# A one-element memset and a wait for it after every second indirect DMA of GpSimd

## What is computed

```python
edge_index = jnp.stack([src, dst])
x = x + _L0_gnn_ref(_layernorm(x), edge_index, W, a)            # graph attention
x = x + _L0_ffn_ref(_layernorm(x)[None], ...)[0]                # top 1 of 32 experts
x = x + _L1_gnn_ref(_layernorm(x), edge_attr_8, edge_attr_4, ..., edge_index)
x = x + _L1_ffn_ref(_layernorm(x)[None], ...)[0]                # top 2 of 6 experts
x = x + _L2_gnn_ref(_layernorm(x), src, dst, ...)               # Q, K, V attention on edges
x = x + _L2_ffn_ref(_layernorm(x)[None], ...)[0]                # 8 experts, dense
x = x + _L3_gnn_ref(_layernorm(x), W, att, src, dst)            # attention of 4 heads
x = x + _L3_ffn_ref(_layernorm(x)[None], ...)[0]                # top 2 of 8 experts
```

```python
z = jnp.einsum('nd,hdf->nhf', h, W)
e = jax.nn.leaky_relu(es[src] + ed[dst], SLOPE)
ex = jnp.exp(e - m[dst])
alpha = ex / safe                                               # safe: sum of ex per target
out = jax.ops.segment_sum(alpha[:, :, None] * z[src], dst, num_segments=N)
```

## Time and profile before

| | us |
|---|---|
| median of 3 runs | 5434.05 |
| fastest and slowest run | 5420.24, 5452.84 |
| span of the profiled execution | 5506.1 |
| PE busy in it | 3864.8 (70%) |
| DVE busy | 3234.8 (59%) |
| ACT busy | 2686.0 (49%) |
| POOL busy, 2641 instructions | 2546.9 (46%) |

### The profile page before, as it was taken

How to read it: one execution, slowest core, us unless ns; L and a number is a source line. 1 busy time by engine, 2 the same in 40 slices (tenths; PEclk the granted TensorE clock), 3 DMA queues, 4 the chain that set the end, 5 groups by cost and what they waited for, 6 DMA issues and landing times.

```text
span 5506.1 us, 74255 instructions
## 1 busy us (share of the span) xinstructions
PE 3864.8 (70%) x19152; PEld 2551.9 (46%) x19152; DVE 3234.8 (59%) x8314; ACT 2686.0 (49%) x8902; POOL 2546.9 (46%) x2641
## 2 busy tenths in 40 slices
PE   5767888822428999977766666668999936556665
PEld 2336656612314444456634444445555524444454
DVE  7864666514246889876566777764333335555753
ACT  5644666611116888863335555553333325555521
POOL 5655555553346777713425555532000046666234
PEclk8977898855668999988878888889999966677778
DMA  3013232312223333323335555550000023333334
GB/s 116 22 45 82 76 77 78 76 15 64 78 63 91 89 86 88 85 25 110 109 124 147 145 150 142 147 133 1 6 12 12 10 80 82 87 86 88 38 112 131
DMA packets 278819, 441.36 MB, mean 80 GB/s; under 512 B 114083, under 2 KB 192781, under 8 KB 278157
## 3 DMA queue, kind: packets, MB, share of 16 engines
q0 software_dynamic: 124624, 331.70, 23.7%
q1 hardware_dynamic: 147230, 98.37, 6.2%
q10 hardware_dynamic: 6560, 6.55, 0.4%
HBM read 368.84 MB, written 67.60 MB: 79 GB/s over the span
## 4 chain that ended last, share of the span: by engine, by line
PE 49%; DVE 16%; another core or an unknown queue 15%; issue 9%; ACT 7%; DMA 2%; DVEq 1%; POOL 0%; ACTq 0%; SPq 0%; POOLq 0%
PE PB L3144 6%; PE PB L2528 6%; PE PB L726 5%; PE PB L1998 5%; PE PB L1079 4%; PE PB L3128 3%; ACT XNT L2612 2%; PE PB L2008 2%; PE PB L1574 2%; PE PB L1088 1%; PE PB L1562 1%; DVE bigt L705 1%; PE PB L2020 1%; PE PB L2015 1%
## 5 line engine op out<-in xcount | busy, mean ns | idle before, releaser
L2528 PE MATMUL PB<-XNT 128*128 128x260 f32 x1760 | 605.0, 480 | 115.8 <-DVE bigt L2500 51.7
L2646 POOL DMA_INDIRECT bigt<-ZTAB,DO x440 | 459.8, 1045 | 270.7 <-issue 122.7
L1023 POOL DMA_INDIRECT bigt<-HTAB,bigt x440 | 419.9, 954 | 350.3 <-ACT bigt L1109 203.5
L1970 POOL DMA_INDIRECT bigt<-YTAB,bigt x440 | 469.4, 1067 | 141.7 <-issue 128.3
L717 ACT ACTIVATE bigt<-bigt 128x128 f16<-128x128 f16 x1214 | 383.2, 389 | 230.6 <-PE PB L726 89.1
L726 PE MATMUL PB<-bigt 128*128 128x440 f16 x1564 | 386.3, 376 | 132.7 <-issue 67.3
L359 POOL DMA_INDIRECT RECS<-bigt x391 | 383.4, 980 | 188.2 <-issue 102.3
L2528 PEld LDWEIGHTS PB<-XNT 128*128 128x128 f32 x1760 | 371.9, 234 | 195.8 <-DVE XNT L2408 59.3
L2612 ACT ACTIVATE XNT<-bigt 128x65 f32<-128x65 f32 x1768 | 446.2, 336 | 0.0
L705 DVE TENSOR_SCALAR bigt<-PB,bigt 128x440 f16<-128x440 bf16 x782 | 315.5, 440 | 222.3 <-PE PB L726 151.4
L2646 POOL DMA_INDIRECT bigt<-KVTAB,DO x296 | 281.7, 952 | 336.0 <-DVE XNT L2408 169.7
(11 more groups left out here) (490 smaller groups left out, 9398.9 us busy)
## 6 DMA issues: line engine op xcount, KB each, us to landing
bigt<-YTAB,bigt POOLq DMA_INDIRECT x552
bigt<-SRT SPq DMA_DIRECT2D x56, 128.0 KB
OUTS<-bigt SPq DMA_DIRECT2D x56, 128.0 KB
SRT<-bigt SPq DMA_DIRECT2D x11, 640.0 KB, 9.9
bigt<-HTAB,bigt POOLq DMA_INDIRECT x440
bigt<-ZTAB,DO POOLq DMA_INDIRECT x440
KVTAB<-bigt SPq DMA_DIRECT2D x25, 258.0 KB
YTAB<-bigt SPq DMA_DIRECT2D x10, 640.0 KB, 9.9
```

The source lines that it names most:

```text
L1023: e.indirect_dma_start(out=Gt[:, g % GB, j, :], out_offset=None, in_=HTAB, in_offset=bass.IndirectOffsetOnAxis(ap=SO[:, g * G + j:g * G + ...
L1970: e.indirect_dma_start(out=Gt[:, g % GB, j, :], out_offset=None, in_=YTAB, in_offset=bass.IndirectOffsetOnAxis(ap=SO[:, g * G + j:g * G + ...
L2528: m = e.matmul(self.PV[n % len(self.PV)], self.OH[:, g % 2, j, :], self.msg[:, g % 2, j, :], start=(k == 0), stop=(k == self.H - 1))
L2646: e.indirect_dma_start(out=dst[:, j, :], out_offset=None, in_=table, in_offset=bass.IndirectOffsetOnAxis(ap=DO[:, g * G + j:g * G + j + 1] ...
```

## The change

A new tile `still` of one float32 on one partition, and a helper `pause`, which sets it to zero on POOL and lets POOL wait for that write. It is called after every second indirect DMA, in the routed row moves of the `direct` branch after every scatter and every second gather, and in `gather_rows` after its two. The gathers of L1734 get none. Whatever else an indirect DMA waited for stands as before.

```diff
--- before.py
+++ after.py
@@ -120,6 +120,7 @@
         ones = sb("ones", [128, 128])
         tri = sb("tri", [128, 128])
         padf = sb("padf", [128, 1])
+        still = sb("still", [1, 1])
         real = sb("real", [128, 1])
         stats = sb("stats", [128, NT, 6])
         mv = sb("mv", [128, NT, 2])
@@ -340,6 +341,11 @@
             m = recs_out[piece % 2]
             return m.sem, m.base + 16 * sum(min(EC, q * PIECE + PIECE) - q * PIECE for q in range(piece % 2, piece + 1, 2))
 
+        def pause(e):
+
+            e.memset(still[:, :], 0.0).then_inc(Q.up(), 1)
+            e.wait_ge(*Q.now())
+
         def attr_load(e, piece, landed):
             c0, c1 = piece * PIECE, min(EC, piece * PIECE + PIECE)
             e.dma_start(ATTR[:, piece % 2, 0:c1 - c0, :], A["attr12"].rearrange(
@@ -359,6 +365,8 @@
                 e.indirect_dma_start(
                     out=RECS, out_offset=bass.IndirectOffsetOnAxis(ap=APOS[:, c:c + 1].bitcast(U32), axis=0),
                     in_=ATTR[:, piece % 2, k, :], in_offset=None).then_inc(recs_out[piece % 2].sem, 16)
+                if c % 2:
+                    pause(e)
                 recs_next[0] = c + 1
 
         bn = {}
@@ -1024,6 +1032,8 @@
                             out=Gt[:, g % GB, j, :], out_offset=None, in_=HTAB,
                             in_offset=bass.IndirectOffsetOnAxis(ap=SO[:, g * G + j:g * G + j + 1].bitcast(U32), axis=0),
                         ).then_inc(gathered.sem(g), 16)
+                        if j % 2:
+                            pause(e)
 
             def pe_dst(e, i):
 
@@ -1714,6 +1725,8 @@
                                 out=xin[:, s % NB, :], out_offset=None, in_=YTAB,
                                 in_offset=bass.IndirectOffsetOnAxis(ap=inverse.source[:, s:s + 1].bitcast(U32), axis=0),
                             ).then_inc(fetched.sem(s), 16)
+                            if s % 2:
+                                pause(e)
                     return
                 attr_scatters(e, 78)
                 e.wait_ge(*begun.last)
@@ -1724,6 +1737,8 @@
                         out=SRT[0:NS * 128, :],
                         out_offset=bass.IndirectOffsetOnAxis(ap=pos[:, t:t + 1].bitcast(U32), axis=0),
                         in_=xs[:, t, :], in_offset=None).then_inc(rows_out.sem, 16)
+                    if t % 2:
+                        pause(e)
                 attr_scatters(e, 78)
                 e.wait_ge(*rows_out.last)
                 for end in stored.ends:
```

## The result

The changed kernel takes 5467.57 us in the median (5458.01 to 5479.67, 4 runs), the kernel before in the same runs 5430.68 (5420.24 to 5452.84): ratio 1.0061, 95% interval 1.0039 to 1.0083. It is 0.6% slower where I had forecast 7.4% faster.

What follows compares the result with a forecast made beforehand. TensorE's completions, late beside POOL's unbroken indirect DMAs, were taken to bound the kernel. 5506 us - 412 lateness + 7 for pauses = 5101, times 0.987 = 5034 us, 7.4% less; range 4870 to 5380 us.

Steps and rivals of the forecast that it cites:

- What bounds the kernel: Whole chain: TensorE's completions arrive late while POOL issues unbroken indirect DMAs; unknown entry 14.8%, 815 us.
- The price of a pause: POOL's gap between two DMAs: +0.06 us per pause, bounds -0.04 and +0.30; 75 us more on POOL.
- Nearly all beside waits of its own: POOL's 75 us more in gathers, scatters and routed loops: mostly covered by its waits, +7 us on the path.
- A POOL instruction that is no DMA lets the completions through. The pause puts one after every second: All POOL's DMA runs: inferred from L1_gnn's COPY between groups of four gathers; lateness taken away, 412 us.
- 412 us: Lateness removed over all stages: 487 us summed, less 75 deducted because L1_gnn with its break still shows 3.5%.
- rival 1: Break too short, or COPY is not what saves L1_gnn: only the +7 us remain, 5441 us; chance 0.05.
- 102 us: Second run of scatters: lateness in the chain as 88.6% of 115 us, of which 85 us was taken.
- Rival 2: L1_gnn and routed loops: pause dear at +0.30 us and buys nothing, 44 us slower, 5478 us; chance 0.07.
- 9 us: L1_gnn under rival 2: growth from 220 pauses at +0.30 us, less 57 us that POOL has to spare.
- Rival 3: POOL's DMA runs: memset written while the DMA before is still being prepared, run unbroken, 5434 us; chance 0.04.
- The rule: Skill's rule against the forecast: nothing of TensorE could hang on POOL's DMAs; only pauses added, ending at rival 1.

Runs made afterwards that it cites:

- q_nowait: All 1255 memsets, each waiting only for the memset two before, against the kernel before on a late chip (5438.75 us): 1.0004.
- p_scat: Pauses only in the attribute scatters and the sorted scatter (207 of 1255), against the kernel before on a prompt chip (4678.15 us): 1.0024.
- p_ffn: Pauses only in the routed row moves of L1_ffn and L3_ffn (168 of 1255), against the kernel before on a prompt chip (4678.15 us): 1.0021.
- s_each: The single pause after every DMA, against the kernel before on a late chip (5501.60 us): 0.9952.
- s_long: The change with a memset of 128x128 in place of the one element, against the kernel before on a late chip (5501.60 us): 0.9872.
- q_full: The whole change run again, against the kernel before on a late chip (5438.75 us): 1.0046.
- q_null: Tile and helper present but no pause called, against the kernel before on a late chip (5438.75 us): 1.0002.
- t_three4: Three pauses in a row after every fourth DMA, against the kernel before on a late chip (5438.37 us): 0.9627.
- u_five4: Five pauses in a row after every fourth DMA, against the kernel before on a late chip (5495.20 us): 5181.33 us, 0.9426.
- q_twice: Each pause of the change twice in a row, against the kernel before on a late chip (5438.75 us): 5279.09 us, 0.9706.
- four parts: Pauses only in scatters, L0/L1 gathers, L2/L3 gathers or routed row moves, against the kernel before on a prompt chip: 1.0024, 1.0028, 1.0029, 1.0021.

## Why the prediction was wrong

**What bounds the kernel.** Right for the chip of the trace: TensorE's completions come late beside POOL's DMAs, and breaks long enough to lift most of it gain 5.7%, near the 7.4% forecast. Whether TensorE's product or only its signal is late the profile cannot tell, since it models the ends of matmuls. Incomplete in what I could not see from one trace: it is no trait of the kernel. On two chips the same program shows no late completion and takes 4680 us.

**The price of a pause**, +0.06 us. Right as the median, 0.09 and 0.27 us between the DMAs, 0.36 in all, and in the gathers of the prompt chip; q_nowait puts it on the wait. Too low among the scatters: 0.2 to 0.3 us on a late chip, where POOL's own completions are late too, and some 0.1 us on the prompt one (p_scat's two runs last 106.4 and 103.7 us, p_ffn's without a pause 101.9 and 99.9). I had put the 39 pauses of a run at 2 us; they took 7 and 9, beside waits that covered them.

**"Nearly all beside waits of its own", on the path +7 us.** Wrong in size. By the medians the change costs 27 and 37 us on the late chips and some 47 on the prompt chip. I had counted POOL's waits for ScalarE's L1109 and VectorE's L2500 as cover. They are no slack of the stage. As I read the code, POOL, ScalarE and VectorE wait for one another in a ring, so a delay of POOL's comes back to it; what the profiles show is 18 us more in L3, and 9 in L0 that may be chance. No run tries the ring by itself. I had also put the pauses at the start at nothing since POOL waits 27 us before its first gather; the first gather came 5.9 us later.

**"A POOL instruction that is no DMA lets the completions through. The pause puts one after every second", 412 us.** This is the step that failed. The chain's unknown entry stayed (14.8 to 14.9%), and none of the 412 us came. It is not enough that an instruction of another kind stands between the DMAs: a pause adds 0.06 us to every second gap, the spacing of the gathers goes from 1.25 to 1.28 us, and nothing changes. Lateness went when POOL's DMAs were spread to 1.43 us (7.0% unknown) and 1.50 us (2.8%); the same memset and wait five times over after every fourth DMA bring 5.7%, most of what I had forecast of one. I had read it from L1_gnn, where a COPY with a break of 0.39 us stands after four gathers and 3.5% is unknown. By the table breaks of that size do little (s_each, s_long), so L1_gnn must be spared for another reason. I had named one in rival 1, that PE's work there hangs on few round trips; no run has tried it, and it stays open. The trace had the warning, and I had put it into rival 1: after the scatters it took 10 us until the first step, so a third of a microsecond was little. One of the readings behind the 412 us was also too high: the shares of the second run of scatters add up to over 100% in its row (88.6% and 24.8% are the first two), so 102 us is no clean figure for it. That did not decide anything.

**The rivals.** Rival 1 is what happened, at 5441 forecast and 5467.57 measured: the break is too short. Rival 2 (5478) lies nearer in time, but by another mechanism: the memsets were not lengthened (94 ns in the mean) and L1_gnn did not grow by 9 us (677.8 us in q_full, 676.1 in q_null). Part of it did come, though, elsewhere: DMAs after a memset that started late, among the scatters. Rival 3 is excluded, the memsets start at their DMA's end.

**The rule.** The Trainium skill ("SBUF — State Buffer", section "Who interferes with whom") knows only the port pair of VectorE and GpSimd as a place of contention and says that PE never waits on anyone. The prompt chips agree: 202 matmuls in 90 us beside unbroken scatters. On the late chips TensorE's completions do depend on POOL's DMAs, 44 matmuls and 182 on one chip with nothing changed but the breaks. The rule is on ports of SBUF and does not tell what they share there, and no run here does.

Of the range: 4870 to 5380 left the result out by 88 us. I gave rival 1 a chance of 0.05 with one row for the break's length and none for its effect. With a mechanism read from a correlation between stages, and the length of the break unproven, it should have had several times as much.

## What to carry to other kernels

Where a profile puts a tenth or more of a one-core kernel's chain into an unknown queue, look whether GpSimd issues indirect DMAs without a break there, and time the kernel on another chip before mending it: here that alone was 14%. A pause does not work by being there; it has to take DMAs out of POOL's time, here a seventh to a fifth more time from one to the next (1.43 and 1.50 us for 1.25). On late chips breaks of 1.0 and 1.3 us after every fourth DMA gained 3.7 and 5.7%; the doubled pause after every fourth, which gained 1.9% there, cost 4.4% on a prompt chip. None of the versions that ran on both kinds beats the kernel before on both; t_three4, u_five4 and q_twice, the best on late chips, did not run on a prompt one. The pause of 0.36 us after every second DMA loses on late chips, and on the prompt chip each of its four parts loses.

## What the runs showed of the hardware that I had not expected

- Two kinds of chips for one program: 5431, 5439, 5502, 5438 and 5495 us for the kernel before on five occasions, 4678 and 4681 on two, with nearly equal durations of POOL's DMAs (952 and 954 ns, 959 and 968 ns). The last four of the five and the two were on six different chips.
- On a late chip it is not TensorE alone that is heard late. In q_nowait POOL's own memsets are late among the scatters; each waits for the one two before it:

```profile
1132.06 0.09 POOL L351 MEMSET still<- 1x1 f32 x1 [0.48 <-remote]
...
1136.26 0.09 POOL L351 MEMSET still<- 1x1 f32 x1 [1.64 <-remote]
...
1141.85 0.09 POOL L351 MEMSET still<- 1x1 f32 x1 [3.04 <-remote]
```

The third waits 3.04 us for the first, which had ended at 1132.15, 9.7 us ahead. In the change, where POOL stops and waits for each at once, 0.27 us is the rule, and the longest among the scatters is 3.29 us.

- Beside unbroken scatters TensorE gets through one matmul in 2 us on a late chip (44 in 90 us); with breaks of 0.95 us after every fourth one in 0.44, and on a prompt chip one in 0.45 without a break.
- A DMA behind two memsets starts 0.62 us after the last one in the gathers of L0, L2 and L3, but 0.27 us in L1's and 0.28 in most of the first run of scatters (medians of q_twice; a quarter of all its scatters behind a pause have 0.63 or more); behind a single one the median is 0.27 or 0.28 everywhere. I had expected 0.27 throughout and have no reason for it.
